# Global attention: the transposed row maxima go through the exponentials' PSUM ring instead of the maxima's own banks

## What is computed

```python
x = x + _L0_attn_a_ref(_layernorm(x, axis=-1), ...)      # attention in groups of 64 tokens
x = x + _L0_ffn_ref(_layernorm(x, axis=-1), ...)
x = x + _L0_attn_b_ref(_layernorm(x, axis=-1), ...)      # "global attention"
x = x + _L0_ffn_ref(_layernorm(x, axis=-1), ...)

def _L0_attn_b_ref(x, Wq, Wk, Wv, Wo, lambda_q1, ..., subln_g):   # per sequence: s = 1024
    q = rope((x @ Wq).reshape(b, s, 32, 8)); k = rope((x @ Wk).reshape(b, s, 32, 8))
    v = (x @ Wv).reshape(b, s, 16, 16)
    probs = softmax(q k^T * 8 ** -0.5)                   # 32 heads of 1024 x 1024 scores
    w = probs[first of a pair] - lam * probs[second of a pair]
    attn = w @ v                                         # then RMS norm, gain, @ Wo
```

## Time and profile before

| | |
|---|---|
| median of 3 runs | 8452.06 us (8442.98 to 8460.63) |
| span of the profiled execution | 8446.8 us |
| busy share of the span | PE 91%, DVE 82%, ACT 75%, POOL 38% |
| costliest groups | DVE row maxima 4708.3 us, ACT exponentials 4406.7 us, PE values 2623.5 us, PE max scores 2490.0 us, PE exp scores 2487.6 us |

### The profile page before, as it was taken

How to read it: one execution, slowest core, us unless ns; L and a number is a source line. 1 busy time by engine, 2 the same in 40 slices (tenths; PEclk the granted TensorE clock), 3 DMA queues, 4 the chain that set the end, 5 groups by cost and what they waited for, 6 DMA issues and landing times. The chain is left out here.

```text
span 8446.8 us, 166394 instructions
## 1 busy us (share of the span) xinstructions
PE 7668.1 (91%) x65600; PEld 2778.4 (33%) x65600; DVE 6929.7 (82%) x8963; ACT 6349.5 (75%) x11710; POOL 3201.4 (38%) x4546
## 2 busy tenths in 40 slices
PE   6899988999889998899988999889998999989999
PEld 3322343223432234322343223432234322343223
DVE  5899768997689976899768997689966899668996
ACT  3699756997569975699756997569975699756996
POOL 3244232442334423344233442334423344233441
PEclk9999999999999999999998999999999999989999
DMA  0100001000010000100001000010000100001000
GB/s 30 46 21 22 18 11 46 21 25 15 11 46 22 24 15 11 46 25 21 15 12 46 24 21 15 11 50 21 25 16 6 50 21 25 20 3 50 25 21 21
DMA packets 219183, 205.49 MB, mean 24 GB/s; under 512 B 108086, under 2 KB 143414, under 8 KB 218358
## 3 DMA queue, kind: packets, MB, share of 16 engines
q1 hardware_dynamic: 218364, 194.46, 8.0%
HBM read 123.83 MB, written 67.37 MB: 23 GB/s over the span
## 5 line engine op out<-in xcount | busy, mean ns | idle before, releaser
L1467 DVE TENSOR_REDUCE mfull<-ps 128x1 f32<-128x1024 f32 x4096 | 4708.3, 1217 | 331.9 <-PE ps L1389 331.1
L1542 ACT ACTIVATE work<-ps 128x512 f32<-128x512 f32 x8192 | 4406.7, 598 | 371.5 <-PE ps L1411 255.2
L1429 PE MATMUL ps<-work,vbuf 128*32 128x256 f32 x32768 | 2623.5, 392 | 119.5 <-ACT hh L1562 119.5
L1389 PE MATMUL ps<-kop,qop 48*128 48x512 bf16 x8192 | 2490.0, 386 | 48.8 <-DVE mfull L1467 23.7
L1411 PE MATMUL ps<-qop,kop 51*128 51x512 bf16 x8192 | 2487.6, 384 | 0.4 <-DMA qop<-mT 0.2
L1429 PEld LDWEIGHTS ps<-work,vbuf 128*32 128x32 f32 x32768 | 654.3, 108 | 1767.9 <-issue 966.8
L1411 PEld LDWEIGHTS ps<-qop,kop 51*128 51x128 bf16 x8192 | 481.8, 93 | 1639.4 <-ACT work L1542 1525.0
L1493 POOL CAST mpart<-mfull 128x16 bf16<-128x16 f32 x256 | 50.5, 197 | 2472.0 <-issue 2005.6
L253 POOL TENSOR_TENSOR rstd<-rstd,nhalf 128x8 f32<-128x8 f32 x64 | 109.2, 1707 | 1644.4 <-DVE rstd L247 1644.4
L445 POOL TENSOR_TENSOR hh<-work,hmask 128x1024 f32<-128x1024 f32 x256 | 521.0, 2062 | 447.4 <-POOLq L1663 329.0
L1511 POOL TENSOR_TENSOR work<-work,none 128x16 f32<-128x16 f32 x224 | 650.8, 2906 | 17.9
(11 more groups left out here) (185 smaller groups left out, 9042.3 us busy)
## 6 DMA issues: line engine op xcount, KB each, us to landing
qop<-scratch SPq DMA_DIRECT2D x512, 64.0 KB
scratch<-work SPq DMA_DIRECT2D x32, 768.0 KB, 4.1
scratch<-hh SPq DMA_DIRECT2D x32, 768.0 KB, 3.6
kop<-scratch SPq DMA_DIRECT2D x256, 96.0 KB
vbuf<-in_x SPq DMA_DIRECT2D x9, 2048.0 KB, 8.3
qop<-scratch SPq DMA_DIRECT2D x512, 32.0 KB
kop<-scratch SPq DMA_DIRECT2D x256, 64.0 KB
qop<-mT SPq DMA_DIRECT2D x1024, 3.0 KB
```

What stands on the lines that cost most here:

```text
L1389: pe.matmul(ps[:, b + n, :], qop[r:r + KQ, s, i, t * P:(t + 1) * P], kop[r:r + KQ, s, i, half(n)], start=True, stop=True).then_inc(s_ms, 1)
L1429: mm = pe.matmul(ps[VW * i:VW * (i + 1), OB, cols], vp[:, b, t, (G * gl + i) // 2, :], prob[:, u % PS, i, cols], start=t == 0 and part == ...
L1467: v.tensor_reduce(mfull[:, m // CUT % 2, r // ROWS * G // 2 + i, to:to + 1], ps[:, b:b + NB, :].rearrange("p b n -> p (b n)"), AX.X, ALU.m ...
L1542: act.activation(prob[:, u % PS, hl, :], ps[:, EB[slot % len(EB)], :], ACT.Exp, scale=scale).then_inc(s_ex, 1)
```

## The change

The transposed maxima get a slot of their own in the ring of the exponentials' banks. `maxima_slot(h)` is this slot, one after both exponentials of step 16h - 5, and `slot_of` and `turn_slot` count the slots that maxima take. The semaphores `s_mt` and `s_mts` go: the transpose increments `s_sc` as an exponentials' matmul does, ACT's copy increments `s_ex` as an exponential does. `MAXIMA` lists the same steps as before. The instructions of every engine stay in their order; what changes is the bank and what is waited for.

```diff
--- before.py
+++ after.py
@@ -1260,7 +1260,6 @@
             s_ms = sem("da_ms")
             s_mr = sem("da_mr")
             s_mc = sem("da_mc")
-            s_mt, s_mts = sem("da_mt"), sem("da_mts")
             s_sc, s_ex, s_pv, s_oe = sem("da_sc"), sem("da_ex"), sem("da_pv"), sem("da_oe")
             s_ch = sem("da_ch")
             DMAS = 2 * (len(Q_ROWS) + len(K_ROWS))
@@ -1277,6 +1276,7 @@
             HEADS = (0, 2, 1, 3)
             HQ = HALF // 2
             EARLY = [STEPS * (g + 1) + o for g in range(FIRST) for o in (9, 25)]
+            MAXIMA = [CUT * (h + 1) - 1 + TURN - AHEAD for h in range(NB * GROUPS)]
             LATE = [STEPS * (FIRST + 1) + o for o in (16, 20)]
             scale = DD ** -0.5
 
@@ -1290,17 +1290,17 @@
                 u, hl = k // G, HEADS[k % G]
                 return u, u // (NB * T), u // T % NB, u % T, hl
 
-            def turns_until(e):
-
-                return sum(1 for s in EARLY if s <= e)
-
             def slot_of(k):
 
-                return k + turns_until(k // NB)
+                return k + sum(1 for s in MAXIMA if s < k // NB) + sum(1 for s in EARLY if s <= k // NB)
 
             def turn_slot(j):
 
-                return NB * EARLY[j] + j
+                return NB * EARLY[j] + sum(1 for s in MAXIMA if s < EARLY[j]) + j
+
+            def maxima_slot(h):
+
+                return NB * max(MAXIMA[h] + 1, 0) + sum(1 for s in EARLY if s <= MAXIMA[h]) + h
 
             def max_bank(m):
 
@@ -1313,8 +1313,7 @@
 
             def turn_at(h):
 
-                m = CUT * (h + 1) + TURN
-                return m, ps[0:PARTS * CUT, max_bank(m), 0:P // 2].bitcast(BF16)
+                return ps[0:PARTS * CUT, EB[maxima_slot(h) % len(EB)], 0:P // 2].bitcast(BF16)
 
             def placed(h):
 
@@ -1351,7 +1350,7 @@
                     def maxima(g):
                         s = g % SLOTS
                         for n in range(NB):
-                            sp.wait_ge(s_mts, NB * g + n + 1)
+                            sp.wait_ge(s_ex, maxima_slot(NB * g + n) + 1)
                             for side in range(2):
                                 for i in range(G // 2):
                                     r0, k = ROWS * side + KQ, PARTS * T // 2 * (side * G // 2 + i)
@@ -1384,18 +1383,15 @@
                             pe.wait_ge(s_op[s], 16 * DMAS * (g // SLOTS + 1))
                         if m >= 2 and n == 0:
                             pe.wait_ge(s_mr, m - 1)
-                        if m % CUT == TURN and n == 0 and m >= CUT:
-                            pe.wait_ge(s_mts, m // CUT)
                         pe.matmul(ps[:, b + n, :], qop[r:r + KQ, s, i, t * P:(t + 1) * P],
                                   kop[r:r + KQ, s, i, half(n)],
                                   start=True, stop=True).then_inc(s_ms, 1)
 
                     def turn_maxima(h):
                         pe.wait_ge(s_mc, CUTS * (h + 1))
-                        m, turned = turn_at(h)
-                        pe.wait_ge(s_mr, min(m - 1, LAST))
-                        pe.transpose(turned, mpart[:, :, :, :].rearrange("p h s t -> p (h s t)"),
-                                     identb[:, :]).then_inc(s_mt, 1)
+                        bank_for(maxima_slot(h))
+                        pe.transpose(turn_at(h), mpart[:, :, :, :].rearrange("p h s t -> p (h s t)"),
+                                     identb[:, :]).then_inc(s_sc, 1)
 
                     def bank_for(slot):
                         if slot >= len(EB):
@@ -1435,7 +1431,7 @@
                     for e in CLOCK:
                         if value_tile(e) is not None:
                             project_values(pe, value_tile(e))
-                        if e == 0:
+                        if e == MAXIMA[0]:
                             pe.wait_ge(s_ve, TT // 2)
                         if e in EARLY:
                             early_turn(EARLY.index(e))
@@ -1444,14 +1440,14 @@
                                 exp_scores(NB * e + n)
                             if e + AHEAD < LAST:
                                 max_scores(e + AHEAD, n)
-                        if at(e, TURN) is not None:
-                            turn_maxima(at(e, TURN))
+                        if e in MAXIMA:
+                            turn_maxima(MAXIMA.index(e))
                         for part in range(2):
                             if tile_due(e, part) is not None:
                                 values(tile_due(e, part), part)
                         if e in LATE:
                             if e == LATE[0]:
-                                pe.wait_ge(s_mts, NB * GROUPS)
+                                pe.wait_ge(s_mr, LAST)
                                 pe.wait_ge(s_oe, NB * (FIRST + 1))
                             turn_output(pe, LATE.index(e))
 
@@ -1489,7 +1485,7 @@
 
                         pool.wait_ge(s_mr, CUT * (h + 1))
                         if h >= 1:
-                            pool.wait_ge(s_mt, h)
+                            pool.wait_ge(s_sc, maxima_slot(h - 1) + 1)
                         link(pool.tensor_copy(mpart[:, :, 0, :], mfull[:, s]))
                         link(pool.tensor_tensor(mrem[:, 0], mfull[:, s], mpart[:, :, 0, :], ALU.subtract))
                         link(pool.tensor_copy(mpart[:, :, 1, :], mrem[:, 0]))
@@ -1551,10 +1547,10 @@
                         act.copy(raw[j % 2], src[:, :, 0:LD + 1]).then_inc(s_ex, 1)
 
                     def keep_maxima(h):
-                        act.wait_ge(s_mt, h + 1)
+                        act.wait_ge(s_sc, maxima_slot(h) + 1)
                         if h >= 1:
                             act.wait_ge(s_md[(h - 1) // NB % SLOTS], placed(h - 1))
-                        act.copy(mT[:, :], turn_at(h)[1]).then_inc(s_mts, 1)
+                        act.copy(mT[:, :], turn_at(h)).then_inc(s_ex, 1)
 
                     def keep_output(u):
                         g, n = u // (NB * T), u // T % NB
@@ -1568,8 +1564,8 @@
                         if 0 <= e < LAST:
                             for n in range(NB):
                                 exponentials(NB * e + n)
-                        if at(e, TURN) is not None:
-                            keep_maxima(at(e, TURN))
+                        if e in MAXIMA:
+                            keep_maxima(MAXIMA.index(e))
                         if tile_due(e, 1) is not None and tile_due(e, 1) % T == T - 1:
                             keep_output(tile_due(e, 1))
 
```

## The result

The changed kernel takes 8342.97 us (median of 4 runs, 8331.17 to 8360.41) against 8448.26 us before (median of 4 runs). The ratio is 0.9873 with a 95% interval of 0.9856 to 0.9890: 1.3% faster, where 8350 us had been forecast. The profiled execution spans 8329.3 us, 117.5 us less than the one before.

What follows compares the result with a forecast made beforehand. PE's matmuls were taken to bound the block, with DVE's wait at the turn lost to everyone. 30 x 0.41 + 0.5 - 0.1 = 12.7 us a round, 102 us in eight, gave 8350 us; range 8325 to 8390.

Steps and rivals of the forecast that it cites:

- What paced the block: Steady block: PE's matmuls set the pace, 1.107 us a step; DVE needs 18.1 us of the 19.51 us period.
- The removed wait: At the turn's transpose: without the wait for DVE the next step starts at 2504.72 instead of 2505.20, gaining 0.48 us.
- the other wait: Max scores behind the turn: their wait on ACT's copy of mT goes; no size was given.
- its picture: Last turn of a round, without max scores beside it: transpose 0.53 us into the step, which takes 1.27 us.
- The added waits: Ring slots at the turn: transpose 0.05 us late, next step's second exponentials' matmul 0.04 late, leaving 0.41 us gained a turn.
- The DMAs: Between ACT's copy of mT and its first use: the nearest limit behind the gain, still hidden by 0.08 us.
- The floor of 4.31 us: Shortest time from ACT's copy to the matmul needing it, from the last turn; PE can come at most 0.49 us earlier.
- The rival: At step 16h: copy's DMAs land later, perhaps for operand loads, and take the gain back; 8404 us, chance 0.08.
- The ends of a round: First turn gains 0.5 us a round (bounds 0 and 0.69); last turn loses 0.1 us a round.
- POOL's cut: At the transpose: if POOL's parts, not DVE, ended last in most turns, nothing is freed; 8452 us, chance 0.04.
- The clock: Steady block: PE's short pauses while the turn holds a bank bring a 1.2 GHz clock; 8554 us, chance 0.04.
- some 90: Profile after: DVE's total idle time falls by some 90 us, all of it at the turns.

Runs made afterwards that it cites:

- Experiment 1: Changed kernel with the transpose's old wait on DVE put back: 8423.82 us, ratio 0.9971 to the kernel before.
- experiment 2: Changed kernel with the max scores behind a turn waiting again for ACT's copy of mT: 8443.25 us, ratio 0.9997 to the kernel before.
- Experiment 5: Changed kernel with the transpose placed behind the values of its step instead of before them: 8342.27 us, ratio 0.9879 to the kernel before.
- experiment 7: Changed kernel with AHEAD 21 instead of 23, maxima turned two steps closer to their first use: 10534.37 us, ratio 1.2465 to the kernel before.
- experiment 4: Changed kernel with TURN 2 instead of 3, so transpose, slot and copy stand one step earlier: 8397.76 us, ratio 0.9942 to the kernel before.
- experiment 6: Changed kernel with the turn at the head of its step on PE and ACT: 8356.08 us, ratio 0.9886 to the kernel before.
- experiment 3: Changed kernel with both removed waits put back, only the slot in the exponentials' ring kept: 8446.62 us, ratio 0.9999 to the kernel before.
- experiment 8: Changed kernel with a new output's first values product behind the next step's first exponentials' and max matmuls: 8343.89 us, ratio 0.9869 to the kernel before.

## Why the prediction was right

**What paced the block.** The prediction took PE's matmuls as the pace, with DVE and ACT having room. After the change DVE's reductions run in longer chains without a PE row that waits for them at the turn (the row of eleven tiles above), and the steps beside the turn keep their 1.107 us ((2497.89 - 2494.57) / 3).

**The removed wait.** The last turn of a round was used as the picture of an unhindered one. Experiment 1 shows that the wait for DVE alone is worth 0.35 us a turn, experiment 2 that the gain needs the other wait's removal as well. The prediction said of that one only that it was lost; it did not give it a price, and the price is the whole gain. The prediction's sum was right because both went: its picture, a turn with no max scores beside it, has neither wait, so that the second was in the 0.48 us without being named. In that part the right number is owed to the choice of the picture and not to an account of this wait.

**The added waits.** 0.05 for the transpose and 0.04 for the second matmul were expected, 0.41 us gained; measured were 0.07 (S + 0.60 against 0.53) and 0.02, and 0.43 gained. The exponential in front of the transpose ends at 2491.98 + 0.59 = 2492.57, S + 0.45 and not the worked-out 0.43, and the transpose follows it by 0.15 us, as the prediction had taken from DVE. Experiment 5 shows that they don't add up in this way: without the first, the second takes its place. The latency of 0.05 us between an exponential's end and the matmul is right. A small term was missing: the max scores' extra wait instruction, about 0.02 us of the difference (in the kernel before, the step behind the turn takes 2506.33 - 2505.20 = 1.13 us and not 1.107). 240 x 0.43 = 103 us less the 5 us of step 240 are the 98 us measured in the block; the sum had 240 x 0.41 = 98.

**The DMAs.** The floor of 4.31 us stood up to experiment 7, and 4.38 us after the change keep clear of it, by 0.07 us where 0.08 had been expected. The rival was nevertheless real at one turn in 32. The operand loads, which the prediction named as its reason, are in the queue at every second turn, but the landing is late only where a packet of instructions falls in the same time. The trace shows that experiments 4 and 6, with a step or nearly one more of lead, don't wait there. The 2 us a DMA that the prediction cites were measured on DMAs issued by GpSimd (the Trainium skill, "DMA: Bandwidth & Descriptors", Anatomy of one DMA); here SP issues, and no run priced a single one.

**The ends of a round.** Expected 0.5 - 0.1 us; up to the first exponentials the gain is 0.7 us, and what of it the half clock takes back cannot be told, since the time at half clock behind it differs by more than that between rounds (7.3 to 10.7 us in the changed kernel). The prediction's 0.5 is not shown.

**The other rivals.** POOL's cut was not last, but it is next: experiment 4. The clock stayed at 1.00 over the steady stretch. DVE's idle time fell by 110 us and not by some 90: 240 turns of 0.41 us are already 98, and the beginnings of the rounds add to it. The Trainium skill's rule of a clock that oscillates when PE cycles through banks ("TensorE: Matmul & The Clock Gate", A second HAM failure mode: psum-queue depth-cycling) does not show in the pauses of this kernel, before or after (granted clock 1.00 over 489.5 and 450 us). Pauses of 6.2 us, in experiment 7, did bring the half clock (0.53).

**The total.** 102 us were forecast and 105.3 lie between the medians. In the profiled pair it is 117.5, of which 8.4 are in unchanged stages and 5 in one round's scratch writes; the traces of the experiments differ there by up to 30 us, so a forecast to within 10 us could not be tested on totals. The periods of the block, which repeat within 0.01 us, are what the reasons were tested on.

## What to carry to other kernels

Where a small job borrows a buffer from a stream, it waits for the reader of that stream, here for DVE, one tile behind. A slot in another ring, whose reader is further ahead, can free it; the place itself is worth nothing (experiment 3), only the waits that go with it. Two waits in a row hide each other: one that shows no idle time in the profile can be worth as much as the one that does, and each must be priced as if the other were gone. Before a job is moved by a step, look at what stands ahead of it in the fixed order of every engine that feeds it, as POOL's chain of 9 us does here.

## What the runs showed of the hardware

- A matmul starts 0.05 us after the end of the instruction that it waits for: after ACT, after POOL (2490.98 to 2491.03 in experiment 4), and after DVE (2614.66 to 2614.71 in experiment 8). At the turn of the kernel before 0.15 us passed behind DVE, and in experiment 2 2492.07 - 2491.93 = 0.14 behind ACT's copy. In these two places the wait is an instruction of its own in PE's queue, of 0.05 us, ahead of the weight load:

```profile
L1396 PEldq EVENT_SEMAPHORE  x256: 51/51/51, 348.9 to 8285.7; - x128
```

- That two semaphores are waited for does not by itself cost the longer time: the transpose of experiment 4 waits for ACT in such an instruction and for POOL in its own weight load, and it follows POOL, the later of the two, by 0.05 us.
- Four DMAs of 3 KB, issued one after the other by SP, make their data usable 4.29 to 4.33 us after the start of the ACT copy that they wait for (4.31 at the earlier trace rows, 4.29 and 4.33 where PE stands still for them in experiment 7; 5.04 at step 240 of the changed kernel, beside a packet of instructions).
